# State-space pass of a decoder layer: who makes the diagonal B tiles, where y is transposed back, and when the convolution taps run

## The reference

```
u = silu(causal_conv4(x @ W_in_u.T) + b_conv)            # 1024 channels
dt, B, C = split(u @ W_xproj.T)                          # 32, 16, 16 columns
delta = softplus(dt @ W_dt.T + b_dt)
h[t] = exp(delta[t] * A) * h[t-1] + delta[t] * u[t] * B[t]   # 1024 x 16 states
y = sum_n(h[t, :, n] * C[t, n]) + D * u
out = (y * silu(res)) @ W_out.T
x = layernorm(x + out)
```

## Time and profile before

| | value |
|---|---|
| timed runs, median (lowest, highest) | 2460.01 us (2459.32, 2470.49) |
| profiled execution, its own time | 2475.47 us |
| span of the profiled execution | 2473.7 us |
| PE busy | 2333.5 us, 94% |
| weight loads (PEld) busy | 1392.6 us, 56% |
| DVE busy | 1852.8 us, 75% |
| POOL busy | 1670.3 us, 68% |
| ACT busy | 1565.1 us, 63% |
| mean granted PE clock | 0.981 |

### The profile page before, as it was taken

The page is one execution under the profiler, slowest core; times in us unless marked ns, Lnnn a source line. Parts: engine busy times, 40 slices in busy tenths (PEclk is TensorE's granted clock), DMA queues, the critical chain, the costliest instruction groups (busy, mean ns, idle before and its releaser), DMA issues. The chain is left out here.

```text
span 2473.7 us, 38405 instructions
## 1 busy us (share of the span) xinstructions
PE 2333.5 (94%) x15232; PEld 1392.6 (56%) x15232; DVE 1852.8 (75%) x2166; ACT 1565.1 (63%) x2604; POOL 1670.3 (68%) x909
## 2 busy tenths in 40 slices
PE   8898999999899999999999999898899999999998
PEld 4565666566566666556666655554545554554553
DVE  4998898898899899889889887772474565466363
ACT  3786887878778788777788877762333343443432
POOL 1898899898899889888989888882432333233130
PEclk9999999999999999999999999998899999999999
DMA  6677978877877878797787777866200100000000
GB/s 207 141 154 161 223 156 177 218 169 164 212 163 171 189 191 168 158 225 160 174 216 164 175 185 180 196 148 170 103 1 34 35 18 18 34 18 1 17 18 17
DMA packets 103525, 329.57 MB, mean 133 GB/s; under 512 B 9571, under 2 KB 46819, under 8 KB 72627
## 3 DMA queue, kind: packets, MB, share of 16 engines
q0 software_dynamic: 27648, 201.34, 41.3%
q1 hardware_dynamic: 75699, 125.78, 14.9%
HBM read 107.25 MB, written 18.51 MB: 51 GB/s over the span
## 5 line engine op out<-in xcount | busy, mean ns | idle before, releaser
L1020 POOL TENSOR_TENSOR mamba_ring<-mamba_ring,mamba_c_row 128x1024 f32<-128x1024 f32 x512 | 1277.0, 2655 | 45.1 <-DVE mamba_ring L908 44.6
L908 DVE TENSOR_TENSOR_SCAN mamba_ring<-mamba_ring,ps 128x512 f32<-128x512 f32 x1024 | 1175.0, 1201 | 141.1 <-PE ps L452 135.7
L713 ACT ACTIVATE mamba_ring<-mamba_delta,mamba_a_neg 128x512 f32<-128x512 f32 x1024 | 660.4, 710 | 91.6 <-DMA mamba_ring<-mamba_ring 90.0
L452 PEld LDWEIGHTS ps<-shared,mamba_v_t 64*128 64x128 f32 x8192 | 501.2, 189 | 257.8 <-issue 148.0
L452 PE MATMUL ps<-shared,mamba_v_t 64*128 64x128 f32 x8192 | 583.4, 285 | 62.1 <-DVE mamba_ring L908 61.0
L1029 POOL DMA_DIRECT2D mamba_ring<-mamba_ring x192 | 181.5, 945 | 154.9 <-DMA mamba_ring<-mamba_ring 130.5
L1703 POOL TENSOR_TENSOR xf_pr<-xf_pr,xf_top 128x1232 f32<-128x1232 f32 x32 | 75.0, 2343 | 255.5 <-DVE xf_top L1602 255.5
L418 PE MATMUL ps<-mamba_xt,mamba_wres 128*128 128x512 f32 x512 | 242.1, 616 | 0.0
L361 PE MATMUL ps<-mamba_xt,mamba_wu 128*128 128x512 f32 x464 | 218.5, 614 | 5.4 <-DMA mamba_xt<-x_t 5.4
L882 DVE SCALAR_TENSOR_TENSOR mamba_u<-ps,mamba_wcv,mamba_u 128x511 f32<-128x511 f32 (+2 forms) x192 | 142.2, 741 | 73.7 <-ACT mamba_u L678 71.2
L504 PE MATMUL ps<-mamba_wout,mamba_u 128*128 128x512 f32 x352 | 167.9, 611 | 0.0
(11 more groups left out here) (150 smaller groups left out, 2859.6 us busy)
## 6 DMA issues: line engine op xcount, KB each, us to landing
mamba_ring<-mamba_ring POOLq DMA_DIRECT2D x192, 1024.0 KB, 7.7
mamba_c_row<-c_rows SPq DMA_DIRECT2D x32, 1024.0 KB, 12.1
mamba_wres<-w_res SPq DMA_DIRECT2D x64, 256.0 KB, 6.5
mamba_wu<-w_u SPq DMA_DIRECT2D x58, 256.0 KB, 4.1
x_rows<-x SPq DMA_DIRECT2D x32, 256.0 KB, 7.5
mamba_xt<-x_t SPq DMA_DIRECT2D x7, 1024.0 KB, 10.7
x<-x_rows SPq DMA_DIRECT2D x28, 256.0 KB, 5.3
xf_xn<-x SPq DMA_DIRECT2D x16, 256.0 KB, 7.8
```

The source lines that it names most:

```text
L452: m = nc.tensor.matmul(ps[:, 2 * s + i, tb * P:(tb + 1) * P], v_t[g % 2][i * H:(i + 1) * H, tb * P:(tb + 1) * P], diag_b[i * H:(i + 1) * H ...
L713: a = nc.scalar.activation(ring[:, q % NR, i, :], delta[:, d % EARLY, :], ACT.Exp, scale=a_neg[:, d, 2 * k + i:2 * k + i + 1])
L908: m = nc.vector.tensor_tensor_scan(ring[:, r, i, :], ring[:, r, i, :], both[:, bass.ds(i, T, 2)], 0.0, ALU.mult, ALU.add)
L1020: nc.gpsimd.tensor_tensor(ring[:, q % NR], ring[:, q % NR], c_row[:, 2 * k:2 * k + 2, :], ALU.mult).then_inc(c_done, 1)
```

## The change

Three things move, all in `mamba_pass`.

1. From block 1 on, ACT makes all eight diagonal tiles: 0, 1, 2, 3 at (7, 1), (7, 2), (7, 3), (7, 6) of the block before, and 4, 5, 6, 7 at (0, 0), (0, 1), (0, 2), (0, 4). Before, ACT made 1, 2, 4 and 5, 6, 7, and DVE made 0 and 3 at (7, 1) and (7, 4).
2. PE's `y_transposes` of a group moves from the end of step 7 to step 0 of the group after, behind its `b_products`.
3. DVE's first two taps move from k = 2 to behind the scan of k = 3 and the third from k = 3 to k = 4; of the second u tile of a group, taps one and two come at k = 7 and the third at k = 0 of the next group, ahead of `gate_y`.

```diff
-    BY_DVE, BY_ACT = (0, 3), (1, 2, 4, 5, 6, 7)
+    BY_ACT = (0, 1, 2, 3, 4, 5, 6, 7)
...
                 if q + 1 < TOTAL:
                     b_products(q + 1)
+                if k == 0 and g >= 2:
+                    y_transposes(g - 2)
...
-                if k == 7 and g >= 1:
-                    y_transposes(g - 1)
...
+            y_transposes(NG - 2)
             pe.wait_ge(scanned, TOTAL)
...
-                if feeds and d == 7 and k in (2, 3, 6):
-                    act_diag(b + 1, {2: 1, 3: 2, 6: 4}[k])
-                if back and d == 0 and k < 3:
-                    act_diag(b, k + 5)
+                if feeds and d == 7 and k in (1, 2, 3, 6):
+                    act_diag(b + 1, {1: 0, 2: 1, 3: 2, 6: 3}[k])
+                if back and d == 0 and k in (0, 1, 2, 4):
+                    act_diag(b, {0: 4, 1: 5, 2: 6, 4: 7}[k])
...
+                if feeds and k == 0 and d - 1 in TWO_U:
+                    conv_tap((b + 1) * ND + FIRST_U[d - 1] + 1, BANK_A, 2)
                 if k == 0 and g >= 2:
                     gate_y(g - 2)
                 if feeds and d < 5:
                     n = (b + 1) * ND + FIRST_U[d]
-                    if k == 2:
+                    if k == 3:
                         conv_tap(n, BANK_A, 0)
                         conv_tap(n, BANK_A, 1)
-                    if k == 3:
+                    if k == 4:
                         conv_tap(n, BANK_A, 2)
-                    if k == 6 and d in TWO_U:
+                    if k == 7 and d in TWO_U:
                         conv_tap(n + 1, BANK_A, 0)
-                    if k == 7 and d in TWO_U:
                         conv_tap(n + 1, BANK_A, 1)
-                        conv_tap(n + 1, BANK_A, 2)
...
-                if feeds and d == 7 and k - 1 in BY_DVE:
-                    make_diag(b + 1, k - 1)
```

More of the change, by code:

```diff
@@ L443, in b_products @@
                         pe.wait_ge(diag_ready, k + 1)
-                    elif k in BY_DVE:
-                        pe.wait_ge(diag_ready, NU + len(BY_DVE) * (b - 1) + BY_DVE.index(k) + 1)
-                    elif k in BY_ACT:
+                    else:
                         pe.wait_ge(diag_act, len(BY_ACT) * (b - 1) + BY_ACT.index(k) + 1)
@@ L894, in make_diag @@
                 dve.wait_ge(bcol_ready, b + 1)
-                if b >= 1:
-                    dve.wait_ge(dbu_ready, (b * ND - 1) * NU + k + 1)
                 nc.vector.tensor_tensor(diag_b[:, :, k], eye2[:].unsqueeze(1).unsqueeze(3).broadcast_to([P, TT, H, 2]),
```

## The result

The changed kernel takes 2472.8 us (median of 20 runs), the kernel before 2464.57 (20 runs). The ratio is 1.0035, 95% interval 1.0022 to 1.0049: a loss of about a third of a per cent, where 38 us of gain were forecast. One run of 6709 us is left out of the ratio. The two profiled executions don't show the loss (2472.1 against 2475.5 us): the timed runs of each kernel spread over 18 to 22 us, and the one profiled before lies 11 us above its median. So what follows compares stretches and not spans, and a difference of a few us between two traces is no measurement. By stretches the traces differ so: block 0 takes 195.1 us for 202.8, blocks 1 to 6 together 3.3 us more, block 7 takes 202.8 for 199.6, and what follows the last scan 793.8 for 796.1.

A forecast was written before the change was run, and what follows sets the result against it. PE was taken as nearly full in block 3 (191.44 of 197.80 us), so only its waits could be won. Terms -25.6 + 6 - 24 = -43.6 us; 2460.0 - 43.6 + 6.4 = 2422.8, rounded to 2422, range 2398 to 2445.

The forecast's parts named there:

- PE is nearly full, and a change can win only what PE waits: Block 3: PE busy 191.44 of 197.80 us, its waits for a scan and for ACT together 6.3 us.
- a floor of 193: POOL's 179.33 us busy plus 11.4 us waiting for DMAs: a block can't fall much below 193 us.
- Slow tiles, -25.6 us: Block ends: four slow DVE diagonal tiles, taken as waits for POOL, go at 6.4 us each; bounds 22.8 to 33.
- the block ends hold the catching up: Long ends 59.22 us against short 52.81 were taken to include what engines catch up after a slow tile.
- Two more tiles on ACT, +6: Group 7's gate comes 2.01 us later, PE stands 1.20 us, seven times; a loss of 6, bounds 0 to 14.
- y transposes and taps, -24: PE's and DVE's waits in blocks 0 to 6: 3.5 us gained in each, 24 in all; bounds 0 to 44.
- P: Theory of the experiments: POOL's products by C plus its waits at merges set a block's time, covering DVE's stalls.
- The wait of `gate_y` for PE not grown: Sign the forecast gave: with y_transposes moved, DVE's wait for PE at gate_y would not grow.
- The tap's wait for ACT: Sign the forecast gave: DVE's wait at a first tap near 0 instead of 7.9 us in a block.
- Timed runs with fewer slow tiles, +6.4: Timed median lay 15.5 us below the profiled execution, so one slow tile's price was taken off the gain.
- The waits only move: Rival: slow tiles go, but the freed 24 us become waits for POOL, a scan or the ring; 2447 us, chance 0.16.
- the slower rival: ACT becomes the bound at block ends, at the gate (7, 4) and tile 7 (0, 4); 2497 us, chance 0.04.

The follow-up runs named there:

- e11: Changed kernel plus a one-column DVE product with two SBUF inputs behind the scan of k = 1 in 63 groups; ratio 1.0454.
- e8: Kernel before, loading only a quarter of C from block 1 on; 2447.1 us, ratio 0.9917.
- e1: Kernel before with only the diagonal tiles changed, ACT making all eight; ratio 1.0009.
- e15: Kernel before with tiles and taps moved, tiles 1 and 2 at (7, 3) and (7, 4), y_transposes and merges left in place; ratio 1.0007.
- e10: Kernel before with tiles and taps moved, y_transposes left at step 7; ratio 1.0017.
- e14: Kernel before with tiles and taps moved, tile 2 made behind group 7's gate, merges at k = 3, 7 and 2, y_transposes left; 2450.9 us, ratio 0.996.
- e5: Changed kernel with POOL's product by C cut to one of two states of a step; 2446.4 us, ratio 0.992.
- e3: Kernel before with only DVE's taps moved; ratio 0.9998.
- e2: Kernel before with only y_transposes moved behind the next group's first product; ratio 1.006.
- e4: Kernel before with y_transposes and taps both moved, the tiles as before; ratio 1.004.
- e9: Changed kernel with gate_y moved from k = 0 to k = 1; median 2466.7 us, ratio 1.0027.

## Why the prediction was wrong

**The views.** "PE is nearly full, and a change can win only what PE waits" left out that POOL's 179.33 us plus its 11.4 at merges are a chain too. I used them as a floor of 193 for one term and not as what the stalls were hidden behind.

**Slow tiles, -25.6 us: the step that failed.** Its reading, a wait for POOL inside the instruction, was right (e11), and so was its price as long as one looks at the block end (e8 has 7 us a block). Wrong was "the block ends hold the catching up": the catching up ran through the whole next block. While DVE stood, POOL worked off its backlog, and the next block then ran free. In the kernel before, POOL's product began on average 0.4 to 2.3 us behind the end of its scan in the groups of blocks 1, 3 and 5, and 1.0 to 6.1 us behind in those of blocks 2, 4 and 6 (starts of L1020 less ends of L908). So 197.8 us of block 3 was not what a block takes without a stall, but what it takes after one. In the changed kernel that lag is 6.2 to 7.0 us in group 0 of each of blocks 1 to 6. The mean of six blocks went from 203.5 to 204.0 us, and the tiles alone gave a ratio of 1.0009 (e1): the term was 0 within the noise. The clock came back only in part: the changed kernel has six stretches at 0.50 between 144.8 and 1503.2 us, 24 us in all, where the kernel before has four, 31 us in all.

**Two more tiles on ACT, +6.** Right in mechanism, and in size as a wait: up to 1.2 us at the gate, 4.9 us in six blocks. In the time it is hidden too (e15 against e10). It shows where nothing else holds group 7: that takes 25.2 us in e1's blocks 3, 4 and 6, and 24.1 us in all of e14's, where tile 2 is made behind the gate.

**y transposes and taps, -24.** Also failed, in two ways. First, P: what was freed went to waits. Second, the sum of the engines' own schedule didn't fall. Per group, medians over blocks 1 to 6 (us between first scans), in kernels where POOL is relieved or, for e3, in its blocks without slow tiles (lowest of six):

| group | 0 | 1 | 2 | 3 | 4 | 5 | 6 | 7 | sum |
|---|---|---|---|---|---|---|---|---|---|
| e8, before with less C | 26.4 | 24.7 | 23.9 | 24.8 | 25.2 | 23.3 | 25.5 | 24.1 | 197.8 |
| e5, changed with half products | 26.0 | 24.1 | 25.3 | 24.3 | 24.8 | 23.4 | 25.9 | 25.2 | 198.9 |
| e3, taps alone | 26.0 | 24.1 | 24.3 | 24.6 | 24.8 | 23.4 | 25.5 | 24.1 | 196.8 |

The taps alone give 1.0 us a block; the rest of the change takes 2.1 back, in groups 2, 6 and 7. "The wait of `gate_y` for PE not grown" failed: I counted what PE would no longer wait for at the transposes (20.8 us in six blocks, and now 4.0) and didn't add the next product's 1.16 us to the path from y to the gate. The tap's wait for ACT, 48.4 us in six blocks, did go, as the sign had it.

**Timed runs with fewer slow tiles, +6.4.** Not needed, as the tiles don't count. Nothing shows that the timed runs had fewer of them; the traces of e2, e3 and e4, which leave these tiles on DVE, have three to five. Some 5 us of the 15.5 lie behind the last scan, nearly all of it the second pass, which no kernel here changes: 796.1 us, where 16 of the other 19 traces have 788.1 to 792.2.

**The rivals.** "The waits only move" named POOL and came nearest in mechanism, but still counted 19.2 us for the tiles; it should have covered both terms. Of the slower rival (ACT at the gate) only the 1.2 us came; the loss of 0.35% came by the y move, which none of my rivals had (e2, e4).

What stays open is how the loss splits within the changed kernel: e2's 0.6% and e10's 0.17% come to more than its 0.35%, so the parts don't add up, and what e9 recovers isn't clear of the noise.

## What to carry to other kernels

A long stall on one engine is worth what the slowest other chain leaves: look, before pricing it, who catches up meanwhile, and whether the fast periods are fast only because they follow a stall. The mean over a whole cycle (203.5 us) is the measure, not its shorter half (197.8). An in-order queue that stands at its own transfers can set the time though it is busy for only 88% of it (180.3 of 203.9 us). There, moving the wait can pay (merges one step later, 0.4%, with y left in its place) where speeding up the others doesn't; but it gave nothing in the changed kernel, so it has to be tried in place. And when work is moved behind another instruction, that instruction's time goes onto the path of whoever waits for the moved one.

## What the runs showed of the hardware

A DVE product of a single column with two SBUF inputs took up to 7.84 us while POOL ran element-wise products back to back, and 0.13 us at least, with no POOL product running; a one-column instruction with one SBUF input took 0.12 to 0.13 us in all 63 places. The wait stands inside the instruction's own recorded time and not as idle time before it. Thirty-one of the 63 took over 1 us. In 25 cases it lasted until POOL's run of two to four instructions was over (within 0.03 us), in seven until one instruction was.

A merge of 1 MB took 6.9 us from issue to landing at the quickest (median of blocks 1 to 6: 7.7 us in the kernel before, 7.9 in the changed one). The first merge of a group is issued two steps after the last merge of the group before, in 60 of 63 cases (62 in the changed kernel) while that one is still under way. These took 8.5 and 8.8 us (median), all the others 7.4 and 7.7. The one issued at 852.83 in the changed kernel, behind such a merge and beside 3 MB of loads, took 14.8 us.
